# Two-layer transformer block: layer 0's probabilities times values out of f16 halves for four of its eight groups, a new order of layer 0, and a wider slot that carries the choice

## The reference, cut to what matters

```
x = x + tanh(g_xattn[0]) * L0_xattn(layernorm(x), ctx, masks)   # 32 heads of 8, in 8 groups of 4 heads
x = x + tanh(g_ffn[0])   * L0_ffn(layernorm(x))                  # Hadamard transform, int8 activations, ternary weights
x = x + tanh(g_xattn[1]) * L1_xattn(layernorm(x), ctx)           # 16 heads of 128, self and context, fp8 roundings
x = x + tanh(g_ffn[1])   * L1_ffn(layernorm(x))                  # 8 experts, the best 2 per row

# L0_xattn
scores = where(causal_mask or padding_mask, -inf, q k^T / sqrt(8))
out    = softmax(scores) v                # keys and values shared by the 4 heads of a group
# L1_ffn
logits = xf @ Wr.T
scores, expert = top_k(logits, 2); weights = softmax(scores)
y = sum over e of gate[:, e] * (silu(xf @ Win[e].T) @ Wout[e].T)
```

## Time and profile before

| | |
|---|---|
| time, 3 runs | 1394.3, 1395.46, 1397.05 us; median 1395.46 |
| profiled execution | 1397.21 us, of which the span is 1394.5 us |
| mean granted TensorE clock | 0.975 |
| PE busy | 1286.3 us, 92% of the span |
| DVE, ACT, POOL busy | 1041.1, 920.0, 746.2 us (75%, 66%, 54%) |
| L784, PV | 256 matmuls, 116.0 us busy |
| DMA | 100.36 MB, mean 72 GB/s |

### The profile page before, as it was taken

The page is one execution under the profiler, slowest core; times in us unless marked ns, Lnnn a source line. Parts: engine busy times, 40 slices in busy tenths (PEclk is TensorE's granted clock), DMA queues, the critical chain, the costliest instruction groups (busy, mean ns, idle before and its releaser), DMA issues.

```text
span 1394.5 us, 30383 instructions
## 1 busy us (share of the span) xinstructions
PE 1286.3 (92%) x8880; PEld 938.1 (67%) x8880; DVE 1041.1 (75%) x2393; ACT 920.0 (66%) x3596; POOL 746.2 (54%) x1091
## 2 busy tenths in 40 slices
PE   3899999999997999999999999999899999569991
PEld 2334444444335888888888888888687888459991
DVE  6456666666676888888888888888788888645554
ACT  1245555454567899899998999899788887223330
POOL 3354646464646556665666566656455786323331
PEclk9999999999998999999999999999999999779996
DMA  5432323222212202201221122102222100622225
GB/s 138 111 76 54 72 55 68 59 60 68 47 54 62 80 2 80 80 21 59 79 79 33 46 79 79 50 29 79 80 66 65 43 32 21 272 75 80 85 77 181
DMA packets 145674, 100.36 MB, mean 72 GB/s; under 512 B 68398, under 2 KB 139055, under 8 KB 145585
## 3 DMA queue, kind: packets, MB, share of 16 engines
q1 hardware_dynamic: 136608, 89.28, 22.3%
q0 software_dynamic: 3744, 8.43, 1.7%
q10 hardware_dynamic: 5232, 1.54, 0.5%
HBM read 58.40 MB, written 42.39 MB: 72 GB/s over the span
## 4 chain that ended last, share of the span: by engine, by line
PE 85%; DVE 5%; issue 2%; POOL 2%; DMA 2%; SPq 1%; ACT 1%; POOLq 0%; DVEq 0%; ACTq 0%
PE ps L1381 11%; PE ps L1481 8%; PE ps L1586 8%; PE ps L1537 7%; PE ps L784 7%; PE ps L1445 6%; PE ps L1388 5%; PE ps_H L2179 4%; PE ps_Y L2195 4%; PE ps L1518 4%; PE ps L763 3%; PE ps L762 3%; PE ps L721 2%; PE ps L722 2%; PE ps L640 1%
## 5 line engine op out<-in xcount | busy, mean ns | idle before, releaser
L1430 POOL TENSOR_TENSOR head_rstd<-head_rstd,minus_half 128x4 f32<-128x4 f32 x192 | 224.5, 1169 | 15.1
L1418 ACT ACTIVATE squares<-ps 128x128 bf16<-128x128 f32 x768 | 201.8, 284 | 45.1 <-PE ps L1381 35.3
L1381 PE MATMUL ps<-w_proj_in,xq 128*128 128x512 f16 (+1 forms) x1024 | 210.2, 328 | 6.8 <-ACT headsT L1454 6.8
L1510 POOL TENSOR_TENSOR prob<-prob,rinv 128x512 f32<-128x512 f32 x128 | 138.2, 1080 | 103.7 <-DVE rinv L1505 103.5
L1497 ACT ACTIVATE prob<-ps,nmax 128x128 f32<-128x128 f32 x512 | 182.1, 390 | 10.9 <-DVE nmax L1488 8.7
L1454 ACT ACTIVATE headsT<-ps,l_hln 128x256 f32<-128x256 f32 (+1 forms) x256 | 167.9, 689 | 29.6 <-PE ps L1445 29.6
L1418 ACT ACTIVATION_READ_ACCUMULATOR squares<-ps 128x1 f32 x768 | 165.3, 216 | 0.0
L1438 DVE TENSOR_TENSOR heads_n<-ps,head_rstd 128x512 f32<-128x512 f32 x192 | 131.5, 685 | 24.3 <-POOL head_rstd L1430 24.2
L729 DVE TENSOR_REDUCE nmax<-ps 128x4 f32<-128x512 f32 x128 | 85.1, 683 | 73.0 <-PE ps L722 72.8
L1481 PE MATMUL ps<-headsT 128*128 128x128 f32 x1024 | 136.4, 277 | 1.1 <-DVE probT L1526 0.5
L1381 PEld LDWEIGHTS ps<-w_proj_in,xq 128*128 (+1 forms) x1024 | 100.5, 98 | 53.5 <-issue 7.7
(11 more groups left out here) (306 smaller groups left out, 2778.0 us busy)
## 6 DMA issues: line engine op xcount, KB each, us to landing
slots<-blank_slot SPq DMA_DIRECT2D x12, 1548.0 KB, 7.4
halves<-half_made SPq DMA_DIRECT2D x32, 256.0 KB, 2.6
w_proj_in<-halves SPq DMA_DIRECT2D x16, 512.0 KB, 10.1
taken<-slots SPq DMA_DIRECT2D x23, 258.0 KB, 2.8
w_out_raw<-in_wprojT SPq DMA_DIRECT2D x8, 512.0 KB, 3.8
half_raw<-in_winT SPq DMA_DIRECT2D x16, 256.0 KB, 3.0
half_raw<-in_woutT SPq DMA_DIRECT2D x16, 256.0 KB, 3.1
w_proj_in<-picked SPq DMA_DIRECT2D x8, 512.0 KB, 7.4
```

The costliest lines, as they stand in the source:

```text
L1381: last = e.matmul(out, xq[:, k, which, slot_at], weights(k, hl, c0, n), start=(k == 0 and hl == 0), stop=(k == KD - 1 and hl == 1))
L1418: last = e.activation(squares[:, 4 * n + h, :], A[n][:, h * HD1:(h + 1) * HD1], ACT.Square, scale=HD1**-0.5, accum_out=hss[:, 4 * n + h:4 ...
L1430: e.tensor_tensor(hr[:, four], hr[:, four], t["half"][:, four], ALU.pow).then_inc(g_r[n].sem, 1)
L1510: e.tensor_tensor(prob[:, kind, :, :], prob[:, kind, :, :], spread(rinv[:, kind, :], P), ALU.mult).then_inc(g_p[kind].sem, 1)
```

## The change

Layer 0. For groups 0 to 3 (`SPLIT = 4`) the exponential is taken twice from the same scores, once into f16 (`EH`, `prob_high`) and once into f32 (`EX`). POOL subtracts the f16 from the f32 and writes the rest as f16 over it (`LP`). PV is then two f16 matmuls, into the same output tile, with `v_half`, which holds the high halves of v, the ones, and the low halves of v in columns of their own. VC has three smaller operations in place of one, and NO of groups 0 to 3 has two more (a copy and an add of the low columns). ST waits for both exponentials. `ORDER0` is new on every engine, and so are the steps that one-off pieces stand ahead of, and `MIXED`.

The end. A slot is 259 f32 values, not 516 f16: the 256 values as f16 halves, row number, expert and the exponential of the gap between the two best scores (GE, ACT). The shares are no longer worked out before the experts; each tile works out its own (`aim`, 4 more DVE operations) and the copy of its result scales by it (2 ACT operations for one). `GROUPS` has four groups, GA three operations for six, the table eleven links for thirteen, and `CLOSING` is new. The read back is on two queues (SP and ACT) in 7 runs of 1, 2, 3, 4, 3, 2 and 1 batches, the adding is 14 plain additions, and there are 7 stores.

```diff
 ORDER0 = {
     "tensor": (
-        "S:7 F5--- ST:4- ST:5- OB:0- NT F6--- P3++ F2t-- ST:6- PV:4- PV:5- ST:7- PV:6- S:0+ F3-- PV:7- "
+        "PV:3- ST:6- NT ST:7- OB:0- F6--- F2t-- P3++ PV:4- PV:5- PV:6- F3-- PV:7- ST:0 S:0+ S:1+ ST:1 "
...
-    "gpsimd": "XB WC F5v--- F4v--- F1g-- MK+ F3b-- F7s--- WL VC+ P1g+++ PD+",
+    "gpsimd": "P1g++++ WL- VC+ F7s--- F4v-- LP:0 LP:1 PD+ F5v-- LP:2 LP:3 F1g- WC F3b- MK+++ XB+++",
...
     @s.piece("VC", "gpsimd")
...
-        e.tensor_tensor(v1[:, p, :, 0:HD0], v_new[:, :, :], v1[:, p, :, 2 * HD0:3 * HD0], ALU.add).then_inc(g_v.sem, 1)
+        e.tensor_tensor(v_half[:, p, :, 0:HD0], v_new[:, 0:SPLIT, :], v1[:, p, 0:SPLIT, 2 * HD0:3 * HD0], ALU.add).then_inc(g_v.sem, 1)
+        e.tensor_tensor(v1[:, p, SPLIT:G0, 0:HD0], v_new[:, SPLIT:G0, :], v1[:, p, SPLIT:G0, 2 * HD0:3 * HD0], ALU.add)
+        e.wait_ge(g_v.sem, g_v.at(i, 1))
+        e.tensor_tensor(v_half[:, p, :, 2 * HD0:3 * HD0], v_new[:, 0:SPLIT, :], v_half[:, p, :, 0:HD0], ALU.subtract).then_inc(g_v.sem, 1)
...
+    @s.piece("EH", "scalar")
+    def _(e, i, p, g):
...
+        e.wait_ge(pe_ST.sem, pe_ST.at(i, g + 1))
+        e.wait_ge(pe_PV.sem, pe_PV.at(i, g - 1) if g >= 2 else pe_PV.at(i - 1, SPLIT - 1 + g))
+        e.activation(high[:, g % 2, :, :].rearrange("p r t -> p (r t)"), ST[g % 2][:, :], ACT.Exp,
+                     bias=pad_bias[:, p:p + 1]).then_inc(a_high.sem, 1)
...
+    @s.piece("LP", "gpsimd")
+    def _(e, i, p, g):
+        e.wait_ge(a_exp.sem, a_exp.at(i, g + 1))
+        e.wait_ge(a_high.sem, a_high.at(i, g + 1))
+        e.tensor_tensor(low(g), prob[:, g % RING0, :, :].rearrange("p r t -> p (r t)"),
+                        high[:, g % 2, :, :].rearrange("p r t -> p (r t)"), ALU.subtract).then_inc(g_low.sem, 1)
...
     @s.piece("PV", "tensor")
...
+        if g < SPLIT:
+            e.wait_ge(a_high.sem, a_high.at(i, g + 1))
+            e.wait_ge(g_low.sem, g_low.at(i, g + 1))
+            e.matmul(O[GP * j:GP * j + GP, :], v_half[:, p, g, :], high[:, g % 2, :, :].rearrange("p r t -> p (r t)"),
+                     start=True, stop=False, tile_position=(0, GP * j))
+            e.matmul(O[GP * j:GP * j + GP, :], v_half[:, p, g, :], low(g),
+                     start=False, stop=True, tile_position=(0, GP * j)).then_inc(pe_PV.sem, 1)
+            return
...
         ahead = {
...
-            ("vector", "P1", 1, 1): ("ready",), ("vector", "WM", 0, 0): ("masks", "late"), ("vector", "MX", 0, 0, 4): ("gated",), ("vector", "P1", 4, 0): ("rows",),
+            ("vector", "P1", 1, 1): ("ready",), ("vector", "P1", 2, 0): ("masks", "gated"), ("vector", "MX", 0, 0, 0): ("late",), ("vector", "P1", 4, 0): ("rows",),
...
-GROUPS = ((0, 10), (10, 14), (14, 16))
+GROUPS = ((0, 10), (10, 12), (12, 14), (14, 16))
...
@@ aim(n), for each tile
+            c_part.link(e.tensor_scalar(both[:, 0, :], second, 1.0, None, ALU.add))
+            c_part.link(e.reciprocal(both[:, 0, :], both[:, 0, :]))
+            c_part.link(e.scalar_tensor_tensor(both[:, 1, :], note[:, :, D + 1:D + 2].rearrange("p s o -> p (s o)"),
+                                               owner[:, n:n + 1], second, ALU.is_equal, ALU.max))
+            e.scalar_tensor_tensor(part[:, n % RING, :], both[:, 1, :], gate[:, 0:1], both[:, 0, :], ALU.mult,
+                                   ALU.mult).then_inc(s_part, 1)
...
+    RUNS = ((0, 1), (1, 3), (3, 6), (6, 10), (10, 13), (13, 15), (15, 16))
...
+                e.tensor_tensor(x[:, b0:b1, :], x[:, b0:b1, :], back[:, which, b0:b1, :], ALU.add).then_inc(s_sum, 1)
```

More of the change, by code:

```diff
@@ L1240, in layer1_attention @@
     total2 = over("o_cols", "total2", [P, 8, P], BF16)
-    catq = sb("catq", [P, 8, P], BF16)
+    catq = over("prob_high", "catq", [P, 8, P], BF16)
     sig = s.flag
@@ L1791, in _ @@
     def _(e):
+        e.memset(shelf_b[:, :], 0.0).then_inc(sets, 1)
+        e.wait_ge(sets, 1)
         for m in range(NE):
@@ L1934, in _ @@
         here = R[:, 0:size * NE]
+        if n == 0:
+            e.wait_ge(sets, 3)
         e.matmul(here, lower[:, :], picks[:, b0:b1, :], start=True, stop=False)
+        e.matmul(here, all_b[:, :], tiled(shelf_b[:, :], size), start=False, stop=False)
         last = e.matmul(here, all_b[:, :], tiled(before[:, :], size), start=False, stop=(size == 1))
@@ L1981, in _ @@
         last.then_inc(s_count, 1)
-    @s.piece("gap", "vector")
-    def _(e):
-        e.wait_ge(makes, 2)
-        e.tensor_tensor(gap[:, 0, :], most[:, 1, :], most[:, 0, :], ALU.subtract).then_inc(s_gap, 1)
-    @s.piece("gap", "scalar")
-    def _(e):
-        e.wait_ge(s_gap, 1)
-        e.activation(gap[:, 1, :], gap[:, 0, :], ACT.Exp).then_inc(s_exp, 1)
+    @s.piece("GE", "scalar")
+    def _(e, n):
+        b0, b1 = GROUPS[n]
+        e.wait_ge(v_gap, n + 1)
+        e.activation(packet[:, b0:b1, D + 2:D + 3].rearrange("p b o -> p (b o)"), gap[:, b0:b1], ACT.Exp).then_inc(a_ge, 1)
     @s.piece("table", "vector")
@@ L2237, in parts @@
                                 ALU.subtract).then_inc(s_hh, 1)
-        t["shares"](e)
+        e.tensor_scalar(gate[:, :], gates[:, 3:4], 1.0 / W_UP, None, ALU.mult).then_inc(s_gate, 1)
         lift(0)
@@ L2264, in _ @@
                 e.wait_ge(put[n % RING], 16 * TS * (n // RING))
-            e.activation(y[:, n % RING, :, :].rearrange("p s d -> p (s d)"), Yb[n % 2][:, :], ACT.Copy).then_inc(s_y, 1)
+            e.wait_ge(s_part, n + 1)
+            for h in range(TS):
+                last = e.activation(y[:, n % RING, h, :], Yb[n % 2][:, h * D:(h + 1) * D], ACT.Copy,
+                                    scale=part[:, n % RING, h:h + 1])
+            last.then_inc(s_y, 1)
     @block.gpsimd
@@ L2276, in _, with read_back @@
                     oob_is_err=False).then_inc(put[n % RING], 16)
-    STEP = 4
+    RUNS = ((0, 1), (1, 3), (3, 6), (6, 10), (10, 13), (13, 15), (15, 16))
     back = t["wout"].bitcast(F32).rearrange("p (w b d) -> p w b d", w=2, b=B)
-    s_back, s_sum, s_store = [sem(f"z_back{n}") for n in range(B // STEP)], sem("z_sum"), sem("z_store")
+    s_back, s_sum, s_store = [sem(f"z_back{n}") for n in range(len(RUNS))], sem("z_sum"), sem("z_store")
+    def read_back(e, which):
+        for n in range(RING):
+            e.wait_ge(put[n], 16 * TS * len(range(n, TILES, RING)))
+        rows = picked.rearrange("(w b p) d -> w p b d", w=2, p=P)
+        for n, (b0, b1) in enumerate(RUNS):
+            e.dma_start(back[:, which, b0:b1, :], rows[which, :, b0:b1, :]).then_inc(s_back[n], 16)
@@ L2281, in _ @@
     @block.sync
     def _(e):
-        for n in range(RING):
-            e.wait_ge(put[n], 16 * TS * len(range(n, TILES, RING)))
-        for n in range(B // STEP):
-            for which in range(2):
-                rows = picked.rearrange("(w b p) d -> w p b d", w=2, p=P)
-                e.dma_start(back[:, which, STEP * n:STEP * (n + 1), :],
-                            rows[which, :, STEP * n:STEP * (n + 1), :]).then_inc(s_back[n], 16)
-        for n in range(B // STEP):
-            e.wait_ge(s_sum, 2 * STEP * (n + 1))
-            e.dma_start(out[STEP * n:STEP * (n + 1)].rearrange("b p d -> p b d"),
-                        x[:, STEP * n:STEP * (n + 1), :]).then_inc(s_store, 16)
```

256 lines of the change are left out of this document (142 added, 114 removed).

## The result

The changed kernel takes 1444.84 us (median of 4 runs, 1436.65 to 1447.33), the kernel before 1395.89 in the same comparison: a ratio of 1.0332 (95% interval 1.0308 to 1.0357). Forecast were 1351 and faster; it is 49 us slower. The profiled execution took 1444.22 us, span 1442.5.

What follows compares the result with a forecast made beforehand. PE was taken to bound the kernel. Layer 0 -44, start +7, closing -4.2 and read back -3.5 sum to -44.7 us: 1397.2 to 1352.5, about 1351 in runs like those shown; 8-in-10 range 1338 to 1372.

Steps and rivals of the forecast that it cites:

- the other engines in a turn: Layer 0 turn: ACT 14.9, DVE 16.4 and POOL 18.3 us of work, all under PE's 20.4.
- the wait of 0.4: Layer 0 turn: PE waits 0.4 us in all for LP and the row maxima, making the turn 20.8.
- GpSimd's times: Layer 0 turn: each LP takes 1.2 us on POOL, whose work rises from 12.87 to 18.3.
- PE's work: Layer 0 turn: packed products in PV cut PE's work by 3.25 us, from 23.66 to 20.4.
- Rival B: Layer 0: the chain of DVE or POOL takes the bound, turn about 22.5 us, 1377 us in total; chance 0.14.
- the 15.5 turns: Layer 0: 2.85 us less per turn over 16 batches less parts in run-in and run-out, -44 us.
- The start: Start of the kernel: P3v(0) waits behind padT, from 17.8 to about 23.9, costing +7 us (+3 to +9).
- The middle: MIXED and layer 1's start: a new weave may give or take 4 us; taken as 0.
- The end: Closing and read back together: -7.7 us, from -4.2 and -3.5.
- the choice's 4.3: Closing: with the choice moved behind catq, catq comes 4.3 us earlier after the last `wide`.
- The read back: After the experts: two load queues and fewer additions, bound by transfers at 385 GB/s, -3.5 us (-2.5 to -5).
- C: Layer 0: every POOL operation is stretched, POOL's 18.3 us becomes 25.4 and sets the turn, 1422 us; chance 0.04.

Runs made afterwards that it cites:

- e2_start: The changed kernel with masks and gated behind the first batch's P3v on VectorE, ahead of P2(2) instead of P1(2); 1436.24 us.
- e11_beside: The kernel before with GpSimd's WC (centring and scaling) moved behind F1g, beside F2 on VectorE; 1396.65 us, ratio 1.0005.
- e3_pool: The changed kernel with GpSimd's WC (centring and scaling) moved behind F3b, not between F1g and F3b; 1413.88 us.
- e7_splitold: The split of PV for groups 0 to 3 put into the order of the kernel before, with the changed kernel's end; 1492.53 us.
- e6_f32: The changed kernel without the split: all eight groups f32, no EH or LP, VC and NO as before, new order kept; 1451.54 us.

## Why the prediction was wrong

The step that failed is the one on the other engines in a turn, "two more 128x128 operations ... 15.83 + 0.6 = 16.4", and with it the wait of 0.4. VectorE's work was summed with durations from the kernel before, where nearly every long operation of GpSimd lay beside idle time or PSUM reads of VectorE. The one exception stood in the rows, L596 at 1.162 against 0.47, and I took it for a general slow-down, not for a matter of place. It is a wait for the end of GpSimd's operation, up to its whole length. Against undisturbed durations it costs L905 1.64, L951 1.24, L603 0.86 and L942 0.4, together 4.1 per turn; L603's counterpart was stretched before too, so 3.5 of it is new. VectorE's busy time in the turn is 19.6 for the 16.4 worked out, and from MX:7 (214.46) to MX:0 (227.55) it takes 13.1 for 10.4 to 11.8. PE's waits came at two places that the prediction did not look at, yn and the bank behind L951, 3.35 where I had 0.4 for LP and the row maxima. The order that I had in hand shows WC between F1g and F3b and WL behind P1g. GpSimd's times were right: LP 1.16 (1.2 taken), turn sum 17.8 (18.3).

The other terms. PE's work: 20.75 (20.4 taken), with the third column tile free and an f16 pair 0.53 to 0.55, as taken. Rival B named the right queue, at 22.5; the turn came out 24.1, and 25.6 where the clock fell, which no case had: in the turns of the kernel before PE did not wait, and its clock was 1.00. The run-out was not priced at all; it lost 13.9 us where the 15.5 turns had it gaining. The start: +7 taken, P3v(0) at 23.76 and masked scores +7.0 as foretold, but how much of the first Wo product's +9.0 is the wait and how much the clock is open (2.8 by the means under e2_start). The middle, "I take 0": +1.6, and +15.5 in layer 1's attention, from WP's place in MIXED and the low clock behind its two waits, which I had not followed at all. The end: -7.7 taken, -4.6 measured; the choice's 4.3 left the stretch from `wide` to catq as foretold, while waits ahead of it grew by 2.8. The read back gave 2.5 of its 3.5 (33.4 us from the last product of the experts to the end, now 30.9); its last store takes 3.3, as it did before, where 2 was taken. C, the only slower rival, had the right sign for another reason: GpSimd's sum stayed at 17.8.

By the runs: order and collision cost most (31 of 49 us back by either of two edits of a few words, some 5 of it at the start by the clock), the late weights about 11. The start's share and the cause of the run-out's loss are not shown. That the clock's falls follow PE's waits is read from the windows, and no run separates it.

## What to carry to other kernels

When an order moves, sum each engine's queue with what the other engine does at the same time, not with means: a VectorE operation such as L905 or L951 beside a long GpSimd operation took until that one ended. Put long GpSimd work beside VectorE's reads of PSUM or its idle time, and look at who waits for VectorE there. Compare two starts only after looking at the clock in both. Price run-in, run-out and every hand-over on their own: a gain per turn times the number of turns holds only for the loop.

## What the runs showed that was not expected

VectorE's operations ended 0.28 to 0.29 us after GpSimd's in four places (L603, L905, L951, and L858 of e11_beside): three SCALAR_TENSOR_TENSOR from SBUF and a TENSOR_SCALAR from f32 to bf16. A TENSOR_TENSOR of 128x1 was held too (L942, 0.59 for 0.16 beside L609). Not every operation from SBUF is: TENSOR_REDUCE L1094 took its 0.94 inside GpSimd's L1106 in e3_pool, and BN_STATS its 0.43 beside L927. Those out of PSUM kept their times.

It is not always VectorE that pays. In e7_splitold GpSimd's L1103 and VectorE's L603 start together:

```profile
194.87 1.82 POOL L1103 TENSOR_TENSOR unit_raw<-unit_raw,unit_sum 128x768 f32<-128x768 f32 x1
194.89 0.47 DVE L603 SCALAR_TENSOR_TENSOR xn<-x_rows,mv_p,rstd_p 128x256 f32<-128x256 f32 x1
```

Here L603 keeps its 0.47, and L1103 takes 1.82 for 1.47. The same stands in three more turns (164.19, 225.56, 287.14), while at 256.92, where L603 had come 0.62 earlier, L1103 takes 1.47. Rival C's stretched row is of this kind: 1.05, and 1.18 for the operation behind it, beside VectorE's L1338 and L1343. Which of two was first, starts 0.02 apart can't tell.

A turn of e6_f32 took 24.76 us at a mean clock of 1.00 and 29.61 at 0.83, with the same work and waits of 2.6 and 2.7: in the longer one the clock was 0.50 from 228 to 236 us, behind the wait that ended at 224.69. Such a wait can cost more by what the clock does behind it than by itself, but it does not do so every time.
